# Two of four heads per group multiply probabilities and values in fp32, the other two split the exponential inside PSUM, and three banks hold scores

## What is computed

```python
# causal: lora_linear for q, k, v and output, T = 224 keys
scores = jnp.einsum('bhqd,bhkd->bhqk', q, k) / jnp.sqrt(jnp.float32(HEAD_DIM))
scores = jnp.where(causal, scores, -jnp.inf)
attn = jax.nn.softmax(scores, axis=-1)
ctx = jnp.einsum('bhqk,bhkd->bhqd', attn, v)
...
# self (224 keys) and cross (750 keys): _mha, residual and layer norm
scores = jnp.einsum('bhqd,bhkd->bhqk', Q, K) / HD ** 0.5
probs = jax.nn.softmax(scores, axis=-1)
ctx = jnp.einsum('bhqk,bhkd->bhqd', probs, V)
```

## Time and profile before

| | |
|---|---|
| median of 3 runs | 3980.43 us (3968.77 to 3981.41) |
| the profiled execution's own time | 3972.95 us |
| its span | 3971.2 us |
| PE busy | 3341.3 us (84%) |
| PEld busy | 2576.8 us (65%) |
| DVE busy | 2893.3 us (73%) |
| ACT busy | 2090.8 us (53%) |
| POOL busy | 866.5 us (22%) |
| mean granted TensorE clock | 0.931 |

### The profile page before, as it was taken

How to read it: one execution, slowest core, us unless ns; L and a number is a source line. 1 busy time by engine, 2 the same in 40 slices (tenths; PEclk the granted TensorE clock), 3 DMA queues, 4 the chain that set the end, 5 groups by cost and what they waited for, 6 DMA issues and landing times. The chain is left out here.

```text
span 3971.2 us, 99389 instructions
## 1 busy us (share of the span) xinstructions
PE 3341.3 (84%) x36576; PEld 2576.8 (65%) x36576; DVE 2893.3 (73%) x4907; ACT 2090.8 (53%) x4472; POOL 866.5 (22%) x802
## 2 busy tenths in 40 slices
PE   7999899588888748888888888988953999999996
PEld 4877778377677636777767777767732556565562
DVE  4767667477777847888888888888855566666666
ACT  2655555355555525666666666666644344343442
POOL 0211111044444500111112121111220212122121
PEclk9999999799989869999999999999956999999998
DMA  3333332233333332333323322323224000000000
GB/s 98 92 101 86 89 100 85 92 102 109 95 101 95 89 112 83 90 95 92 90 86 90 91 83 87 95 85 88 75 89 143 22 22 27 27 22 32 21 22 16
DMA packets 246179, 309.71 MB, mean 78 GB/s; under 512 B 108931, under 2 KB 166275, under 8 KB 245094
## 3 DMA queue, kind: packets, MB, share of 16 engines
q1 hardware_dynamic: 245734, 303.54, 25.7%
HBM read 212.45 MB, written 90.64 MB: 76 GB/s over the span
## 5 line engine op out<-in xcount | busy, mean ns | idle before, releaser
L798 DVE TENSOR_TENSOR cross_p_lo<-cross_p,cross_p_hi 125x448 f16<-125x448 f32 x768 | 559.2, 730 | 140.0 <-ACT cross_p_hi L736 134.7
L735 ACT ACTIVATE cross_p<-cross_ps 125x448 f32<-125x448 f32 x768 | 421.1, 548 | 421.7 <-PE cross_ps L693 406.6
L791 DVE TENSOR_REDUCE cross_mx<-cross_ps 128x1 f32<-128x750 f32 x512 | 475.8, 929 | 28.7 <-PE cross_ps L660 27.3
L736 ACT ACTIVATE cross_p_hi<-cross_ps 125x448 f16<-125x448 f32 x768 | 418.9, 545 | 0.0
L660 PE MATMUL cross_ps<-cross_qk_stack 96*128 96x375 f16 x1024 | 259.2, 335 | 126.3 <-DVE cross_mx L791 125.5
L1244 PE MATMUL ffn_ps_f<-ffn_xt,ffn_f_hi 128*128 128x256 f16 x1792 | 301.8, 276 | 16.5 <-ACT ffn_ht L1316 11.5
L693 PE MATMUL cross_ps<-cross_qk_stack 97*125 97x224 f16 x1536 | 295.0, 275 | 19.1 <-issue 15.6
L585 PE MATMUL cross_ps<-cross_w_hi,cross_ct 128*125 128x128 f16 x3072 | 305.9, 225 | 0.0
L863 POOL TENSOR_TENSOR cross_o_sum<-cross_o_raw 128x256 f32<-128x256 f32 x64 | 41.6, 650 | 1184.9 <-ACT cross_o_raw L742 1184.9
L585 PEld LDWEIGHTS cross_ps<-cross_w_hi,cross_ct 128*125 128x125 f16 x3072 | 294.0, 141 | 0.3
L710 PE MATMUL cross_ps<-cross_vs,cross_p_hi 125*128 125x65 f16 x3072 | 289.2, 193 | 2.7 <-DVE cross_p_lo L798 1.7
(11 more groups left out here) (260 smaller groups left out, 9673.2 us busy)
## 6 DMA issues: line engine op xcount, KB each, us to landing
cross_spill<-cross_proj SPq DMA_DIRECT2D x64, 487.0 KB, 2.9
cross_c_rows<-ctx SPq DMA_DIRECT2D x48, 500.0 KB
cross_qk_stack<-cross_spill SPq DMA_DIRECT2D x128, 187.5 KB, 3.7
cross_qk_stack<-cross_spill SPq DMA_DIRECT2D x64, 243.5 KB, 3.1
causal_spill<-causal_proj SPq DMA_DIRECT2D x64, 224.0 KB, 1.9
causal_qk_stack<-causal_spill SPq DMA_DIRECT2D x256, 56.0 KB, 2.0
self_spill<-self_proj SPq DMA_DIRECT2D x64, 224.0 KB, 2.0
self_qk_stack<-self_spill SPq DMA_DIRECT2D x256, 56.0 KB, 2.0
```

Source lines behind the costliest of these rows:

```text
L735: act.activation(p32[:, n % 2, :], ps_st[0:KC, n % 2, 0:2 * T], ACT.Exp, scale=EXP_SCALE)
L736: act.activation(p_hi[:, n % 4, :], ps_st[0:KC, n % 2, 0:2 * T], ACT.Exp, scale=EXP_SCALE).then_inc(exp_done, 1)
L791: dve.tensor_reduce(mx[:, g, t, h:h + 1], ps_qk[:, :, 0:KT // 2], AX.XY, ALU.max).then_inc(max_done, 1)
L798: dve.tensor_tensor(p_lo[:, n % 4, :], p32[:, n % 2, :], p_hi[:, n % 4, :], ALU.subtract).then_inc(lo_done, 1)
```

## The change

The heads of a group are numbered by slot(n) = 0 or 1 in alternation, and `full_slots=(0,)` in all three phases: slot 0 is full, slot 1 is split. Pairs are reordered, so that even n are full and odd n are split, and a half group (HALF = PAIRS/2 pairs) finishes one head of each kind.

- A full pair: one exponential by ACT, in fp32 (`p_full`); no work on DVE; 4 matmuls by PE with fp32 weights `p_full` (128 queries) and 33 fp32 columns of `vf`, in place of 8 with fp16.
- A split pair: ACT writes `p_hi` first, and then the fp32 exponential over the scores in PSUM; DVE subtracts with one input in PSUM. PE's matmuls are those of before.
- Scores have three banks (ST_RING). A bank's reuse waits for the probabilities of the pair that held it. The output of a half group takes one bank, and is copied out twice a group (2 x 98 columns each instead of 2 x 260 once).
- A v job writes the full heads' values in fp32 and the split heads' high part with two instructions of ACT; DVE's low part has half the columns. POOL's sum has half the columns, its scaling is two instructions.

```diff
-        ps_proj, ps_qk, ps_st, ps_pv = (ps_all[:, 2 * n:2 * n + 2, :] for n in range(4))
+        ps_proj, ps_qk, ps_st = ps_all[:, 0:2, :], ps_all[:, 2:4, :], ps_all[:, 4:4 + ST_RING, :]
+
+        ps_pv = ps_all[:, 7, 0:2 * OW].rearrange("p (t v) -> p t v", t=2)
...
                 if n == 0 and (g > 0 or b.i is not None or b.first > 0):
-                    yield "evacuate", b + (g - 1) // G, (g - 1) % G, 0
+                    yield "evacuate", b + (g - 1) // G, (g - 1) % G, 1
+                if n == HALF:
+                    yield "evacuate", b, g, 0
...
                 elif kind == "scores":
...
-                    wait(pe, exp_done, done_before(b, g, PAIRS, n, 2))
-                    h, c0 = n // (NCH // 2), 2 * (n % (NCH // 2))
+                    wait(pe, *st_free(b, g, n))
+                    bank = st_bank(g, n)
+                    h, c0 = head(n), chunk(n)
...
                 elif kind == "values":
+                    if n % HALF == 0:
+                        wait(pe, pv_evac, no(b, g, 2, n // HALF))
...
-                    pe.wait_ge(lo_done, no(b, g, PAIRS, n + 1))
+                    pe.wait_ge(*probabilities_ready(b, g, n))
...
+                            if s in full_slots:
+                                last = pe.matmul(ps_pv[:, t, O_AT[s]:O_AT[s] + HD + 1], p_full[:, buf, at:at + P],
+                                                 vf[:, g, c, 2 * full_slots.index(s) + n // HALF, :],
+                                                 start=first, stop=final)
+                                continue
...
                 elif kind == "scores":
                     act.wait_ge(st_full, no(b, g, PAIRS, n + 1))
-                    wait(act, lo_done, done_before(b, g, PAIRS, n, 2))
                     wait(act, pv_done, done_before(b, g, PAIRS, n, 4))
-                    act.activation(p32[:, n % 2, :], ps_st[0:KC, n % 2, 0:2 * T], ACT.Exp, scale=EXP_SCALE)
-                    act.activation(p_hi[:, n % 4, :], ps_st[0:KC, n % 2, 0:2 * T], ACT.Exp, scale=EXP_SCALE
-                                   ).then_inc(exp_done, 1)
+                    scores = ps_st[0:KC, st_bank(g, n), 0:2 * T]
+                    if slot(n) in full_slots:
+                        act.activation(p_full[:, p_buffer(n), :], scores, ACT.Exp, scale=EXP_SCALE
+                                       ).then_inc(exp_done, 1)
+                    else:
+                        act.activation(p_hi[:, p_buffer(n), :], scores, ACT.Exp, scale=EXP_SCALE)
+                        act.activation(scores, scores, ACT.Exp, scale=EXP_SCALE).then_inc(exp_done, 1)
...
-                elif kind == "scores":
+                elif kind == "scores" and slot(n) in split_slots:
                     dve.wait_ge(exp_done, no(b, g, PAIRS, n + 1))
-                    dve.tensor_tensor(p_lo[:, n % 4, :], p32[:, n % 2, :], p_hi[:, n % 4, :], ALU.subtract
-                                      ).then_inc(lo_done, 1)
...
+                    dve.tensor_tensor(p_lo[:, buf, :], ps_st[0:KC, st_bank(g, n), 0:2 * T], p_hi[:, buf, :],
+                                      ALU.subtract).then_inc(lo_done, 1)
...
-        lambda sems: attention(nc, sems, "cross", x2, ctx, x3, ca, [None] * 3, ca_bias, ln2, False),
+        lambda sems: attention(nc, sems, "cross", x2, ctx, x3, ca, [None] * 3, ca_bias, ln2, False, (0,)),
```

More of the change, by code:

```diff
@@ L48 @@
 VW = 2 * HD + 1
+ST_RING = 3
 FF = 2048
@@ L179, in vector, with attention @@
             dve.scalar_tensor_tensor(lo, stage, S_W, hi, ALU.mult, ALU.subtract).then_inc(self.w_lo_done, 1)
-def attention(nc, sems, tag, x_in, kv_in, x_out, w, loras, biases, norm, causal):
+def attention(nc, sems, tag, x_in, kv_in, x_out, w, loras, biases, norm, causal, full_slots):
     NB = x_in.shape[0]
@@ L194, in attention @@
     PAIRS = NCH // 2 * GH
+    HALF = PAIRS // 2
+    split_slots = [s for s in range(2) if s not in full_slots]
+    N_SPLIT, N_FULL = len(split_slots), len(full_slots)
+    O_WIDTH = [HD + 1 if s in full_slots else VW for s in range(2)]
+    O_AT = [0, O_WIDTH[0]]
+    OW = sum(O_WIDTH)
     st = ExitStack()
@@ L401, in epilogue @@
         def epilogue():
-            yield "evacuate", Batch(NB - 1), G - 1, 0
+            yield "evacuate", Batch(NB - 1), G - 1, 1
             for g in sorted(OUT_JOBS):
@@ L445, in no, with slot, head, chunk @@
             return b.val(lambda k: (G * k + g) * per_unit + n)
+        def slot(n):
+            return n % HALF % 2
+        def head(n):
+            return n // HALF + 2 * slot(n)
+        def chunk(n):
+            return n % HALF // 2 * 2
+        def p_buffer(n):
+            return n % 4 if N_SPLIT != 1 else n % 4 // 2
+        def split_no(g, n):
+            return (g * PAIRS + n) // (2 // N_SPLIT) + 1
+        def probabilities_ready(b, g, n):
+            if slot(n) in full_slots:
+                return exp_done, no(b, g, PAIRS, n + 1)
+            return lo_done, b.val(lambda k: G * k * PAIRS * N_SPLIT // 2 + split_no(g, n))
+        def st_bank(g, n):
+            m = g * PAIRS + n
+            return 1 if not cross and m == G * PAIRS - 1 else m % ST_RING
+        def st_free(b, g, n):
+            m = g * PAIRS + n
+            back = next(d for d in range(1, G * PAIRS) if st_bank(0, (m - d) % (G * PAIRS)) == st_bank(g, n))
+            if m < back and b.i is None and b.first == 0:
+                return exp_done, 0
+            past = m - back
+            return probabilities_ready(b + (past // (G * PAIRS)), past // PAIRS % G, past % PAIRS)
         def done_before(b, g, per_unit, n, ring):
@@ L728, in perform @@
                     act.wait_ge(proj_full, b.val(lambda k: job_index[kind, k, g] + 1))
-                    out = destination(kind, b, g, 0)[0]
-                    act.mul(out, source(kind, b, g, bank), job_scale(kind)).then_inc(proj_hi, 1)
+                    out, src = destination(kind, b, g, 0)[0], source(kind, b, g, bank)
+                    if kind[0] == "v":
+                        if N_FULL:
+                            c0, c1 = (0, min(4, NCH)) if kind == "v0" else (4, NCH)
+                            last = act.mul(vf[:, g, c0:c1, 0:2, 0:HD], slot_heads(src, full_slots[0:1]), RESPLIT)
+                        if N_SPLIT:
+                            last = act.mul(out, slot_heads(src, split_slots), RESPLIT)
+                        last.then_inc(proj_hi, 1)
+                    else:
+                        act.mul(out, src, job_scale(kind)).then_inc(proj_hi, 1)
```

110 lines of the change are left out of this document (69 added, 41 removed).

## The result

The changed kernel takes 4077.22 us (median of 4, 4075.19 to 4089.15) against 3980.47; the ratio is 1.0256, 95% interval 1.0229 to 1.0284. It is slower by 2.6%. Forecast were 4040 us and slower.

What follows compares the result with a forecast made beforehand. PE becomes the bound, its added fp32 loads outweighing the waits removed. Cross +41, self -19 and causal +46 sum to +68 us on the profiled 3973, so 4041, said as 4040 us; range 3890 to 4170.

Steps and rivals of the forecast that it cites:

- What bounds: PE and DVE near their limit in cross, PE alone in causal; at most 171, 90 and 41 us recoverable (cross, self, causal).
- Price of an fp32 pair: PE's values of a full pair: 0.82 us, bounded by weight loads, 0.59 more than now; 378 us in all.
- load and stream in sequence: Rival for PE's fp32 matmuls: streaming does not hide behind loading, 1.06 us a pair, +154 us, so 4195; chance 0.11.
- DVE's stretching: DVE's subtraction, blocked by POOL with two SBUF inputs, is never stretched with one in PSUM: 66 us, beside 466 for dropped subtractions.
- third bank: Scores on PE: reusing a bank waits for probabilities that values has already waited for, so 0 us.
- single output bank: PE's second-half values wait for ACT's copy: taken as covered, 0; as a rival +67 us, so 4108, chance 0.08.
- Causal: Causal phase: 76 us of added PE work, less 25 idle time recovered and 5 for clock: +46 us.
- Self: Self phase: 76 us of added PE work, less 62 idle time, 25 clock and 8 drain: -19 us.
- Cross: Cross phase: 227 us of added PE work, less 141 idle time, 30 clock and 15 drain: +41 us.
- clock and drain: PE in cross: fewer waits give back 30 us of time at 1.2 GHz and 15 us of last matmuls' drain.
- The faster side: Rival: waits and low clock in self and cross go almost wholly, over 378 us return; 3936 or 3872 us; chance 0.33.
- The clock rival: Full pairs lower PE's mean clock in attention by 0.1: up to +270 us, so 4310; chance 0.06.

Runs made afterwards that it cites:

- wider streaming: Changed kernel with its fp32 matmuls streaming 66 columns instead of 33, the extra ones written to PSUM columns nobody reads: 4079.2 us, ratio 1.0269.

## Why the prediction was right, and where it was off

The change splits into three parts, each measured by a kernel that has it and one that has not:

| part | from | to | us |
|---|---|---|---|
| subtraction from PSUM | before, 1 | 0.9753 | -98 |
| half-group outputs, third bank, new order (no full head) | 0.9753 | 0.9800 | +19 |
| two of four heads in fp32 | 0.9800 | 1.0256 | +181 |

(The ratios times 3980 us.) Together +102 us. The forecast's own sum was +68; on the median of 3980 us that is 4048, so the 4040 that was said left out the 7 us by which the profiled execution lay under the median.

- **What bounds.** Right: PE was the one that the fp32 work met, and its idle time was what could be recovered. It was, to 62 us in cross, 37 in self and 23 in causal.
- **Price of an fp32 pair.** Right: 0.82 us was taken, 0.81 to 0.87 measured, bounded by the loads as read from L974; the bound of 1.06 us for load and stream in sequence is refuted by the wider streaming. The first load hides only behind a long job, so the mean is nearer 0.84, and 384 pairs in cross add (0.84 - 0.22) x 384, some 238 us rather than 227.
- **DVE's stretching.** Right in mechanism, and in size: the subtraction's instructions take 399 us together where they took 932, 533 us less, of 466 + 66 foretold. DVE's busy time fell by 464 only, since it counts instructions that overlap once; the times of all its instructions fell by 542. With one operand moved, the longest subtraction is 2620 ns with two SBUF inputs and 627 with one, and 2.3% of the time go with it. The SBUF rule of the Trainium skill that the prediction names (page "SBUF — State Buffer", section "Who interferes with whom") agrees with these runs.
- **ACT, third bank, single output bank, POOL.** 0 each in the prediction. The third bank is 0 in the changed kernel (1.0261 against 1.0256), the copy's wait 2 us; but the structure as a whole costs the 19 us of the table, for which the sum had no term. POOL's sum has half the columns and not a quarter fewer, which changes nothing.
- **Causal** +46 foretold, +37 measured; the profiled executions with wider streaming and with two banks have 661 and 660 us of causal where this one has 669, so some 8 us of the 37 are chance. **Self** -19 and -18. In self the sum is right, but its parts were not all foreseen, and the exact agreement is luck: 63 us of idle time came back, as allowed (62), although a second pause of issue of 12 us was added, which I had not foreseen; time at 1.2 GHz fell from 100 to 68 us, which gives back 16 us where I took 25.
- **Cross**, +41 foretold and +92 measured, is the term that was mis-sized. Price 11 us more, as above. Idle time recovered: 181 - 62 = 119 us, where I took 141; 42 us of waits for the max stayed where I had left 30 for everything but issue. The last part is clock and drain, for which I took back 45: from the measured sum, 238 - 119 - 92 = 27. Time at 1.2 GHz went from 143 to 109 us by the trace's records of the clock, down by 34 and not by 60, so about 17 us came back and not 30. The loops did better than that (99 to 54 us), but the last groups of cross, at 1.2 GHz throughout, got longer. First the kernel before, then the changed one (the columns of the earlier trace rows):

```profile
2900.00:2941.00 41.00, 32.32 (x340) 22.55 (x337) 32.12 (x46) 30.01 (x66) 11.37 (x9) 0.50 0.04 13
```

```profile
3003.00:3055.00 52.00, 49.42 (x330) 45.01 (x330) 16.83 (x29) 22.98 (x50) 9.57 (x10) 0.50 0.03 10
```

  Nearly the same number of matmuls takes 11 us longer: an fp32 pair costs 1.65 us at that level, 1.3 us more than an fp16 pair, and not 0.6.
- **The rivals.** The faster side needed over 378 us to come back; what came back is about 295 us (640 pairs at 0.84 - 0.22 = 0.62 us are 397, less the 102 that the kernel lost), near the 310 of the forecast. Load and stream in sequence is refuted. The clock rival is not what happened as a whole (the mean granted clock is 0.941 against 0.931). The single output bank is refuted as a wait; the half-group structure as a whole costs some 19 us. Self has 585 us with it and 571 without, beside a second pause of issue of 15 us that only the first has; what brings that pause, and the rest, was not taken apart.

## What to carry to other kernels

For 33 and 66 columns the price of an fp32 matmul was the load of its weights: price an fp32 stationary operand by its loads (0.11 us a record of 128 columns here, two records a matmul) before trading two fp16 matmuls of 0.03 us for it. It is hidden only as far as the engine idles anyway: in self all of it was, and nothing was gained by it; in cross, of some 238 us that the fp32 pairs add, 154 were left in the time (1349 us with no full head, 1502 with them). When a change bundles several edits, price each by itself: here one operand moved to PSUM gave 2.5% and the rest took 5% back.

## What the hardware showed unexpectedly

After the pause at the end of a loop in cross the granted clock stayed low longest in the kernels with fp32 pairs. The changed kernel around such a pause, first in PE's timeline (the wait in brackets):

```profile
2101.57 0.63 PE L752 MATMUL cross_ps<-cross_qk_stack 97*125 97x224 f16 x2 [3.31 <-issue]
```

and then three stretches behind it (the columns of the earlier trace rows, PEclk third from the end):

```profile
2104.00:2110.00 6.00, 5.71 (x25) 3.50 (x24) 2.32 (x4) 1.34 (x3) 2.03 (x1) 0.50 0.26 75
2110.00:2116.00 6.00, 6.00 (x40) 3.92 (x39) 1.60 (x4) 2.01 (x4) 0.00 (x0) 0.72 0.50 161
2116.00:2122.00 6.00, 6.00 (x75) 5.43 (x74) 3.59 (x5) 2.70 (x6) 0.00 (x0) 1.00 0.27 110
```

The low spells that follow such pauses between the loops' turns last 6.8 us in the kernel before, 10.2 (once 6.8) without full heads, 3.4 to 13.7 in the changed kernel (three of five are 13.7), and 13.7 to 23.9 with all heads full, though PE is busy nearly all the while (5.71 of 6 us). A spell costs about half its length where PE is the bound, as a full pair takes 1.65 us in it and 0.84 outside. The nearest test is the changed kernel with its full heads in fp16: the same order of instructions and the same pause, and spells of 3.4 to 6.8 us. So, as far as one execution of each shows, the fp32 pairs lengthen them; but the kernel without any has longer spells than the one before too, so they are not all of it, and why the clock stays low stays open.
